# Attention A of a transformer block: the writes of the position rows issued by ACT instead of SP

## The chip, the cores and the metric

The kernel runs on one core of a Trainium2 chip. The metric is the device time of one execution in microseconds (us); less is better. The core has TensorE (PE), VectorE (DVE), ScalarE (ACT), GpSimd (POOL) and SyncE (SP), each with its own instruction stream, and 16 DMA engines that move data between the on-chip memory (SBUF) and the device memory (HBM). Matmul results lie in PSUM, in banks of 512 float32 per partition. The engines meet only through semaphores.

## The reference

Four sequences of 2048 rows of width 256 go through attention A, a feed-forward, attention B (causal) and the feed-forward again, each behind a layer norm and added to the residual. The change touches attention A, which has a relative position term:

```python
score = (einsum('bhsp,bhtp->bhst', q + u, k) + relative_shift(einsum('bhsp,htp->bhst', q + v, pos))) / sqrt(16)
out   = einsum('bhst,bhtp->bhsp', softmax(score), val)          # 16 heads of 16, s = t = 2048

def relative_shift(x):                                          # x: b, h, s, s
    x = pad(x, one zero column on the left)                     # rows of s + 1
    return x.reshape(b, h, s + 1, s)[:, :, 1:, :].reshape(b, h, s, s)
```

The shift is a change of row length: rows written with a pitch of 2049 elements are read back with a pitch of 2048.

## The kernel before

A loop over the four sequences holds nine phases with a meeting of all engines between them. In attention A one head is 16 tiles of 128 query rows by 2048 keys, and a sequence has 16 heads, so 256 tiles, and 1024 in the whole run. Tiles are a software pipeline: in step s the engines work on tiles that lie at different distances ahead of s (`R_LEAD` 9, `Z_LEAD` 6, `C_LEAD` 4, `T_LEAD` 2, `V_LEAD` 1).

What happens to one tile n, in order:

- PE makes the position scores of tile n in four chunks of 512 columns (L522, in step n-9: chunk 3 first, then 0, 1, 2). DVE copies chunk 3 from PSUM into the ring `rel` (L693), ACT copies chunks 0, 1 and 2 (L639). The ring has four slots (`RING`), and both wait for `rel_out` of tile n-4 before they write.
- The 128 rows of `rel`, 1 MB, are written to HBM with a row pitch of 2049 elements (`write_rows`, L758 to L765, in step n-9; the semaphore is `rel_out`).
- In step n-6 the shifted rows, 1 MB, are read back into the ring `z` (`read_shifted`, L743 to L756, semaphore `rel_in`). This waits until PE has transposed the tile that held the slot (`t_full[3]` of tile n-4) and until the writes of tiles n and n+1 have landed.
- In step n-4 PE makes the content scores (L534), DVE adds them onto `z` and takes the maximum (L658), POOL subtracts it (L716).
- In step n-2 PE transposes the tile in four groups (`turn`, L541) and ACT takes the exponential of each (L631) into `pT`. The transposes and the position scores share three banks of PSUM (`R_BANK`, `T_BANK`), so PE waits in turn for ACT's exponentials and copies. Then the values (L562), the sum over four row groups (L550) and the division follow.

ACT's order in a step is: four exponentials of tile s+2, then three copies of tile s+9. DVE's is: low half of the scores, the copy of chunk 3, high half, and small work. SP's is: the read of tile s+6, the write of tile s+9, and in 13 of 16 steps parts of the loads for the next heads (64 KB each, `qu`/`k` and `qv`/`pos`, 24 in a head, and one of 256 KB for the values). Before the change every DMA of the kernel is issued by SP, so all of them are in one queue. SP works in order: when the read of a tile waits, the write behind it in the program waits too.

Of the kernel before, what the change touches and what calls it, by code (L numbers as in the profile page):

```python
# [26 lines left out]
P = 128  # L27
# [4 lines left out]
S = 2048  # L32
NT = S // P
# [9 lines left out]
FLAT = S * (S + 1)  # L43
RING = 4
# [10 lines left out]
R_ACT = [0, 1, 2]  # L55
R_DVE = 3
R_FIRST = 3
HB = 4
NB = 2
# [5 lines left out]
Z_LEAD = 6  # L65
R_LEAD = 9
# [13 lines left out]
def program(nc, a, out, nb=4, nh=H):  # L80

    ctx = ExitStack()
    with ctx:
        def sb(name, shape, dt=F32):
            return ctx.enter_context(nc.sbuf_tensor(name, shape, dt))
# [4 lines left out]
        def sem(name):  # L90
            return ctx.enter_context(nc.semaphore(name))
# [8 lines left out]
        rel_d = nc.dram_tensor("rel_rows", (NB, FLAT), F32).ap()  # L100
# [8 lines left out]
        rel = sb("rel", [P, RING, S])  # L109
# [105 lines left out]
        r_copied = [sem(f"r_copied{c}") for c in range(4)]  # L215
        rel_out = [sem(f"rel_out{k}") for k in range(RING)]
# [14 lines left out]
        def settle(e):  # L231

            e.sem_inc(waited, 1)
# [257 lines left out]
        def in_order(e, b, step):  # L491

            def counts(p):
                return Counts(*(e.snap(b * (nh // HB * per) + p * per)
                                for per in (G, G // OB, 16 * G // RING, HB // NB * QK_INC, HB // NB * 16)))

            with e.Fori(0, 1) as p:
                base = counts(p)
                for s in range(-R_LEAD, 0):
                    step(p, base, s, lambda n: n >= 0)  # L500
            with e.Fori(0, GROUPS - 1) as p:
                base = counts(p)
                for s in range(G):
                    step(p, base, s, lambda n: True)
            with e.Fori(GROUPS - 1, GROUPS) as p:
                base = counts(p)
                for s in range(G):
                    step(p, base, s, lambda n: n < G)

        def moved(base, n):  # L510

            return base.moves + 16 * (n // RING + 1)
# [107 lines left out]
        def act_attn_a(e, b):  # L620

            def step(p, base, s, here):

                r, t = s + R_LEAD, s + T_LEAD
                if here(t):
                    if s >= 0:

                        e.wait_ge(AA["pv_done"], base.tiles + (t - 1))
                    for q in range(4):
                        e.wait_ge(t_full[q], base.tiles + (t + 1))  # L630
                        e.activation(pT[:, t % 2, q * CH:(q + 1) * CH], rg[:, T_BANK[q], :], ACT.Exp,  # L631
                                     scale=SCALE).then_inc(p_ready[q], 1)
                if here(r):
                    if s >= 0 or r >= RING:

                        e.wait_ge(rel_out[r % RING], moved(base, r - RING))
                    for c in R_ACT:
                        e.wait_ge(r_full[c], base.tiles + (r + 1))
                        e.activation(rel[:, r % RING, c * CH:(c + 1) * CH], rg[:, R_BANK[c], :],  # L639
                                     ACT.Copy).then_inc(r_copied[c], 1)  # L640

            in_order(e, b, step)

# [81 lines left out]
        def load_pair(e, q, k, q_src, k_src, h, slots, done):  # L725

            for a in slots:
                load_part(e, q, q_src, h, a, QPART[a], done)
                load_part(e, k, k_src, h, a, KPART[a], done)

        def load_v(e, h, hd, done):
            e.dma_start(v_s[hd].rearrange("p t w -> p (t w)"),
                        v_d[bass.ds(h, 1)].rearrange("a p w -> (a p) w")).then_inc(done, 16)

        def sp_attn_a(e, b):

            every = range(SLOTS)
            load_pair(e, qv_s[0], pos_s[0], qv_d, pos_d, 0, every, qv_loaded[0])
            load_pair(e, qu_s[0], k_s[0], qu_d, k_d, 0, every, AA["qk_loaded0"])
            load_v(e, 0, 0, AA["v_loaded0"])  # L740
            load_pair(e, qv_s[1], pos_s[1], qv_d, pos_d, 1, every, qv_loaded[1])

            def read_shifted(p, base, n, fresh, last):  # L743

                k, hd, i0 = n % RING, n // NT % NB, n % NT * P
                if not fresh:

                    e.wait_ge(t_full[3], e.snap(base.tiles + (n - RING + 1)))
                    settle(e)
                e.wait_ge(rel_out[k], e.snap(moved(base, n)))  # L750
                settle(e)
                if not last:
                    e.wait_ge(rel_out[(n + 1) % RING], e.snap(moved(base, n + 1)))
                    settle(e)
                shifted = bass.AP(tensor=rel_d.tensor, offset=hd * FLAT + (i0 + 1) * S, ap=[[S, P], [1, S]])
                e.dma_start(z[:, k, :], shifted).then_inc(rel_in[k], 16)  # L756

            def write_rows(p, base, n):  # L758

                k, hd, i0 = n % RING, n // NT % NB, n % NT * P  # L760
                for c in (R_DVE, R_ACT[-1]):
                    e.wait_ge(r_copied[c], e.snap(base.tiles + (n + 1)))
                    settle(e)
                there = bass.AP(tensor=rel_d.tensor, offset=hd * FLAT + i0 * (S + 1) + 1, ap=[[S + 1, P], [1, S]])
                e.dma_start(there, rel[:, k, :]).then_inc(rel_out[k], 16)  # L765

            def next_heads(p, base, s, final):

                hd, at = s // NT, s % NT
                nxt = (hd + 1) % NB  # L770
                if at in range(1, 7) and not (final and hd + 1 >= HB):
                    if at == 1:
                        e.wait_ge(AA["hi_ready"], e.snap(base.tiles + hd * NT + C_LEAD))
                        settle(e)
                    load_pair(e, qu_s[nxt], k_s[nxt], qu_d, k_d, e.snap(p * HB + (hd + 1)), (at - 1,),
                              AA[f"qk_loaded{nxt}"])
                if at == 7 and not (final and hd + 1 >= HB):
                    e.wait_ge(AA["pv_done"], e.snap(base.tiles + (hd * NT + V_LEAD)))
                    settle(e)
                    load_v(e, e.snap(p * HB + (hd + 1)), nxt, AA[f"v_loaded{nxt}"])  # L780
                if at in range(8, 14) and not (final and hd + 2 >= HB):
                    if at == 8:
                        e.wait_ge(r_full[2], e.snap(base.tiles + (hd + 1) * NT))
                        settle(e)
                    load_pair(e, qv_s[hd % NB], pos_s[hd % NB], qv_d, pos_d, e.snap(p * HB + (hd + 2)), (at - 8,),
                              qv_loaded[hd % NB])

            def step(p, base, s, here):

                n, r = s + Z_LEAD, s + R_LEAD  # L790
                final = not here(G)
                if here(n):
                    read_shifted(p, base, n, s < 0 and n < RING, n % NT == NT - 1)
                if here(r):
                    write_rows(p, base, r)
                if s >= 0:
                    next_heads(p, base, s, final)

            in_order(e, b, step)

# [394 lines left out]
        def _(e):  # L1196
# [40 lines left out]
            with e.Fori(0, nb) as b0:  # L1237
# [3 lines left out]
                sp_values(e, b, "A")  # L1241
                meet_b(e, b, 2)
                sp_attn_a(e, b)
                meet_b(e, b, 3)
                meet_b(e, b, 4)
# [83 lines left out]
        @block.scalar  # L1329
        def _(e):  # L1330
            e.wait_ge(loaded, 16 * LOADS)
            act_project(e, None, "pos")
            meet(e, None, 0)
            with e.Fori(0, nb) as b:
                meet_b(e, b, 1)
                act_norm(e, b, 0)
                act_project(e, b, "A")
                meet_b(e, b, 2)
                act_attn_a(e, b)
                meet_b(e, b, 3)  # L1340
                act_out(e, b, "A")
                meet_b(e, b, 4)
                act_norm(e, b, 1)
                act_ffn(e, b, 0)
                meet_b(e, b, 5)
                act_norm(e, b, 2)
                act_project(e, b, "B")
                meet_b(e, b, 6)
                act_attn_b(e, b)
                meet_b(e, b, 7)  # L1350
                act_out(e, b, "B")
                meet_b(e, b, 8)
                act_norm(e, b, 3)
                act_ffn(e, b, 1)
                meet_b(e, b, 9)
# [86 lines left out]
```

## Time and profile before

| | |
|---|---|
| median of 3 runs | 11704.78 us (11701.66 to 11712.92) |
| the profiled execution | 11740.77 us, its span 11739.0 us |
| granted clock of TensorE, mean | 0.925 |
| busy share: PE, weight load, DVE, ACT, POOL | 82%, 59%, 53%, 57%, 25% |
| attention A of the first sequence | first write of rows issued at 179.4 us, last at 1833.1 us |

The run repeats the same pattern four times, once for each sequence. In the profile's table of 40 slices the long stretches in which the DMA digits are 9 are the four attention A phases; attention B, which moves few bytes, lies between them. A share of busy time over the whole span is therefore a mean over phases with different limits, and what follows is read phase by phase.

### The profile page before, as it was taken

The page shows a single profiled execution, that of the slowest core. Times are in us where ns is not written, and L with a number is a line of the kernel's source. Part 1 is how long each engine was busy: PE and PEld are TensorE (multiplying, and loading weights), DVE is VectorE, ACT ScalarE, POOL GpSimd, SP SyncE. Part 2 cuts the span into 40 slices and gives each one's busy share as a digit, 9 for nine tenths or more (in the row PEclk, how much of TensorE's full clock was granted, in tenths as well). Part 3 has the DMA queues.
Part 4 walks back from the last instruction along what each step waited for, and adds up shares of the span by engine and source line. Part 5 has one row for each costly group of instructions (what it writes and reads, how often), then busy time and mean ns, then how long its engine had stood idle before and what let it go on. Part 6 is the DMA issues. An engine that isn't in the chain of part 4 may idle for free. (4 is left out here: it accounts for less than half of the span.)

```text
span 11739.0 us, 268351 instructions
## 1 busy us (share of the span) xinstructions
PE 9666.4 (82%) x95520; PEld 6878.1 (59%) x95520; DVE 6260.3 (53%) x14730; ACT 6698.0 (57%) x11009; POOL 2935.3 (25%) x3520
## 2 busy tenths in 40 slices
PE   5887888899687788899968878889986787888999
PEld 3555556666455556566635555556664555555666
DVE  3555553675355555376445555537744555553764
ACT  3665664675365666366546656637744565663764
POOL 2333332001233333200123333320012333332001
PEclk8999999899799999999979999999998999999999
DMA  6999993100699999210079999920007999992000
GB/s 233 337 337 335 345 342 118 49 23 19 216 356 328 334 355 346 102 27 24 17 242 339 341 335 344 339 96 25 24 26 256 338 332 326 346 345 86 24 24 26
DMA packets 452690, 2482.16 MB, mean 211 GB/s; under 512 B 78976, under 2 KB 100992, under 8 KB 188864
## 3 DMA queue, kind: packets, MB, share of 16 engines
q1 hardware_dynamic: 451264, 2463.71, 62.1%
q8 instruction: 826, 13.53, 0.5%
q14 instruction: 600, 4.92, 0.1%
HBM read 1280.34 MB, written 1183.07 MB: 210 GB/s over the span
## 5 line engine op out<-in xcount | busy, mean ns | idle before, releaser
L658 DVE CUSTOM_DVE_ANT_0 z<-sc,z 128x1024 f32<-128x1024 f32 x2048 | 2497.0, 1220 | 2356.4 <-DMA z<-rel_rows 1959.4
L716 POOL TENSOR_SCALAR z<-z,nmax 128x1024 f32<-128x1024 f32 x2048 | 2271.2, 1120 | 4649.0 <-DVE nmax L668 4649.0
L631 ACT ACTIVATE pT<-rg 128x512 f32<-128x512 f32 x4096 | 2445.2, 598 | 855.0 <-PE rg L541 796.3
L639 ACT ACTIVATE rel<-rg 128x512 f32<-128x512 f32 x3072 | 1727.0, 596 | 1895.0 <-PE rg L522 1886.7
L522 PE MATMUL rg<-pos_s,qv_s 96*128 96x512 bf16 x4096 | 1646.3, 410 | 1382.2 <-DVE rel L693 1261.7
L541 PE MATMUL rg<-ident,z 128*128 128x128 f32 x16384 | 2597.7, 283 | 87.6 <-issue 78.6
L541 PEld LDWEIGHTS rg<-ident,z 128*128 128x128 f32 x16384 | 2067.8, 146 | 827.4 <-ACT rel L639 259.9
L522 PEld LDWEIGHTS rg<-pos_s,qv_s 96*128 96x128 bf16 x4096 | 487.6, 120 | 1872.7 <-DVE rel L693 1505.8
L1006 DVE CUSTOM_DVE_ANT_0 z<-sc,mask 128x1024 f32<-128x1024 f32 (+7 forms) x1536 | 1359.3, 910 | 229.2 <-PE sc L825 176.0
L945 ACT ACTIVATE pT<-rg 128x512 f32<-128x512 f32 (+3 forms) x1792 | 928.3, 550 | 776.2 <-PE rg L878 763.3
L953 ACT ACTIVATE z<-z,nmax 128x128 f32<-128x128 f32 (+15 forms) x1024 | 1226.7, 1198 | 90.0 <-POOL nmax L971 78.2
L878 PE MATMUL rg<-ident,z 128*128 128x128 f32 x8704 | 1262.6, 290 | 0.0
L562 PE MATMUL op<-pT,xnT 128*32 128x128 f32 x32768 | 1209.3, 292 | 0.0
L878 PEld LDWEIGHTS rg<-ident,z 128*128 128x128 f32 x8704 | 976.1, 145 | 256.5 <-issue 188.7
L562 PEld LDWEIGHTS op<-pT,xnT 128*32 128x32 f32 x32768 | 899.0, 116 | 262.8 <-issue 213.9
L859 PE MATMUL op<-pT,xnT 128*32 128x128 f32 x17408 | 794.3, 284 | 149.1 <-ACT pT L945 45.0
L693 DVE COPY rel<-rg 128x512 f32<-128x512 f32 x1024 | 702.4, 686 | 184.6 <-PE rg L522 141.6
L859 PEld LDWEIGHTS op<-pT,xnT 128*32 128x32 f32 x17408 | 503.8, 111 | 298.7 <-DVE attn L981 120.7
L534 PE MATMUL sc<-k_sb,xnT 96*128 96x512 bf16 x2048 | 652.3, 401 | 0.0
L534 PE MATMUL sc<-xnT 96*128 96x512 bf16 x2048 | 636.0, 392 | 12.6 <-DVE mlo L658 12.6
L700 DVE COPY po_sb<-op 128x128 f32<-128x128 f32 x1024 | 298.9, 292 | 597.6 <-PE op L562 596.7
L1025 DVE COPY pT<-rg 128x512 f32<-128x512 f32 (+3 forms) x768 | 428.7, 558 | 302.2 <-PE rg L878 293.1
(93 smaller groups left out, 8191.7 us busy)
## 6 DMA issues: line engine op xcount, KB each, us to landing
rel_rows<-rel SPq DMA_DIRECT2D x1024, 1024.0 KB, 11.3
z<-rel_rows SPq DMA_DIRECT2D x1024, 1024.0 KB, 9.1
xnT<-qu_parts SPq DMA_DIRECT2D x792, 64.0 KB, 2.3
xnT<-v_heads SPq DMA_DIRECT2D x132, 256.0 KB, 4.2
v_heads<-rel SPq DMA_DIRECT2D x8, 4096.0 KB, 12.5
k_sb<-k_parts SPq DMA_DIRECT2D x408, 64.0 KB, 2.3
qv_s<-qv_parts SPq DMA_DIRECT2D x384, 64.0 KB, 9.5
pos_s<-pos_parts SPq DMA_DIRECT2D x384, 64.0 KB, 10.4
```

What stands on the lines that cost most here:

```text
L522: e.matmul(rg[:, R_BANK[c], :], qv_s[hd][:, i0:i0 + P], pos_s[hd][:, c * CH:(c + 1) * CH], start=True, stop=True).then_inc(r_full[c], 1)
L534: mm = e.matmul(sc[:, c, :], qu_s[hd % NB][:, i0:i0 + P], k_s[hd % NB][:, c * CH:(c + 1) * CH], start=True, stop=True)
L541: mm = e.transpose(rg[:, T_BANK[q], (j - 4 * q) * P:(j - 4 * q + 1) * P], z[:, n % RING, j * P:(j + 1) * P], ident[:, :])
L562: mm = e.matmul(po[32 * g:32 * g + 32, :], v_s[hd % NB][:, j, :], pT[:, n % 2, j * P:(j + 1) * P], start=j < 4, stop=j + 4 >= NT)
L631: e.activation(pT[:, t % 2, q * CH:(q + 1) * CH], rg[:, T_BANK[q], :], ACT.Exp, scale=SCALE).then_inc(p_ready[q], 1)
L639: e.activation(rel[:, r % RING, c * CH:(c + 1) * CH], rg[:, R_BANK[c], :], ACT.Copy).then_inc(r_copied[c], 1)
L658: e.tensor_tensor_reduce(out=zs, in0=scf[:, 2 * half * CH:2 * (half + 1) * CH], in1=zs, scale=1.0, scalar=-3.0e38, op0=ALU.add, op1=ALU.ma ...
L716: e.tensor_scalar(zs, zs, 1.0, nmax[:, n % 2:n % 2 + 1], ALU.mult, ALU.add).then_inc(AA[done], 1)
L859: mm = e.matmul(po[32 * g:32 * g + 32, :], v_s[t // NT % NB][:, j, :], pT[:, t % 2, j * P:(j + 1) * P], start=j < 4, stop=j + 4 >= nj)
L878: mm = e.transpose(rg[:, B_BANK[q], (j - 4 * q) * P:(j - 4 * q + 1) * P], z[:, t % RING, j * P:(j + 1) * P], ident[:, :])
L953: e.activation(z[:, s % RING, 0:w], z[:, s % RING, 0:w], ACT.Exp, bias=nmax[:, s % 2:s % 2 + 1], scale=SCALE).then_inc(BB["exp_done"], 1)
L1006: e.tensor_tensor_reduce(out=z[:, s % RING, c0:c1], in0=scf[:, p0:p0 + c1 - c0], in1=mask[:, S - width + c0:S - width + c1], scale=1.0, sc ...
```

## The change

`write_rows` moves from SP's program to ACT's. ACT issues it at the end of its part of a step, behind its own last copy of the tile, and on its own DMA queue. The two semaphores that it waits for are the same (DVE's copy of chunk 3 and ACT's copy of chunk 2), and so are the bytes and their places. SP keeps the reads and the loads.

```diff
@@ act_attn_a
                         e.activation(rel[:, r % RING, c * CH:(c + 1) * CH], rg[:, R_BANK[c], :],
                                      ACT.Copy).then_inc(r_copied[c], 1)
+                    write_rows(base, r)
+
+            def write_rows(base, n):
+
+                k, hd, i0 = n % RING, n // NT % NB, n % NT * P
+                for c in (R_DVE, R_ACT[-1]):
+                    e.wait_ge(r_copied[c], base.tiles + (n + 1))
+                settle(e)
+                there = bass.AP(tensor=rel_d.tensor, offset=hd * FLAT + i0 * (S + 1) + 1, ap=[[S + 1, P], [1, S]])
+                e.dma_start(there, rel[:, k, :]).then_inc(rel_out[k], 16)
@@ sp_attn_a
-            def write_rows(p, base, n):
...
@@ sp_attn_a, step
-                n, r = s + Z_LEAD, s + R_LEAD
+                n = s + Z_LEAD
                 final = not here(G)
                 if here(n):
                     read_shifted(p, base, n, s < 0 and n < RING, n % NT == NT - 1)
-                if here(r):
-                    write_rows(p, base, r)
                 if s >= 0:
                     next_heads(p, base, s, final)
```

ACT, two steps in the middle of attention A, before (`pT<-rg` is an exponential, `rel<-rg` a copy of position scores; L638 is a semaphore's value being worked out):

```order
L631 ACTIVATE pT<-rg 128x512 [waits t_full3]
L638 REGISTER_ALU [waits rel_out2]
L639 ACTIVATE rel<-rg 128x512 [waits r_full0]
L639 ACTIVATE rel<-rg 128x512 [waits r_full1]
L639 ACTIVATE rel<-rg 128x512 [waits r_full2]
L630 REGISTER_ALU [waits A_pv_done]
L631 ACTIVATE pT<-rg 128x512 [waits t_full0]
```

and the same place now:

```order
L631 ACTIVATE pT<-rg 128x512 [waits t_full3]
L638 REGISTER_ALU [waits rel_out2]
L639 ACTIVATE rel<-rg 128x512 [waits r_full0]
L639 ACTIVATE rel<-rg 128x512 [waits r_full1]
L639 ACTIVATE rel<-rg 128x512 [waits r_full2]
L650 DMA rel_rows<-rel 128x2048 [waits r_copied3,r_copied2]
L630 REGISTER_ALU [waits A_pv_done]
L631 ACTIVATE pT<-rg 128x512 [waits t_full0]
```

The DMA and its two waits stand between the last copy of one step and the first exponential of the next.

SP, the middle of attention A, before (`z<-rel_rows` is the read of shifted rows, the 16x2048 rows are loads for the next head):

```order
L756 DMA z<-rel_rows 128x2048 [waits t_full3,rel_out0,rel_out1]
L762 REGISTER_ALU
L765 DMA rel_rows<-rel 128x2048 [waits r_copied3,r_copied2]
L722 DMA xnT<-qu_parts 16x2048
L722 DMA xnT<-k_parts 16x2048
L756 DMA z<-rel_rows 128x2048 [waits t_full3,rel_out1,rel_out2]
L762 REGISTER_ALU
```

and now:

```order
L766 DMA z<-rel_rows 128x2048 [waits t_full3,rel_out0,rel_out1]
L732 DMA xnT<-qu_parts 16x2048
L732 DMA xnT<-k_parts 16x2048
L758 REGISTER_ALU
L766 DMA z<-rel_rows 128x2048 [waits t_full3,rel_out1,rel_out2]
```

The write and its wait are gone from between the reads; reads and loads keep their order.

## Rows read from the trace of the kernel before

**Rows 1.** The page's slices: busy tenths of the DMA engines, and their GB/s
```profile
DMA  6999993100699999210079999920007999992000
GB/s 233 337 337 335 345 342 118 49 23 19 216 356 328 334 355 346 102 27 24 17 242 339 341 335 344 339 96 25 24 26 256 338 332 326 346 345 86 24 24 26
```
**Rows 2.** Busy time by stretch: two of attention A, then one of attention B
```profile
core 0: us, PE busy (x) PEld busy (x) DVE busy (x) ACT busy (x) POOL busy (x), PEclk, DMA share, GB/s
600.00:1200.00 600.00, 481.74 (x5252) 344.65 (x5242) 322.56 (x680) 361.27 (x635) 200.88 (x182) 0.93 0.98 335
1200.00:1800.00 600.00, 484.93 (x5413) 347.04 (x5416) 332.67 (x700) 371.31 (x653) 206.29 (x186) 0.96 1.01 344
1900.00:2400.00 500.00, 445.63 (x3805) 315.77 (x3807) 269.39 (x721) 273.95 (x395) 61.50 (x147) 0.94 0.12 39
```
**Rows 3.** Who waited for whom, whole run: total us, times, longest us
```profile
DVE z L658 <- DMA z<-rel_rows: 1959.4, 820, 9.4
ACT rel L639 <- PE rg L522: 1886.7, 1776, 11.2
DVE z L658 <- PE sc L534: 394.9, 222, 12.7
```
**Rows 4.** The same view for SP's queue, whole run
```profile
SPq L233 <- DMA rel_rows<-rel: 2376.5, 903, 6.7
SPq L233 <- ACT rel L639: 1048.5, 837, 4.2
SPq L233 <- PE rg L541: 841.7, 763, 9.0
```
**Rows 5.** The page's DMA issues: KB each, median us from issue to landing
```profile
rel_rows<-rel SPq DMA_DIRECT2D x1024, 1024.0 KB, 11.3
z<-rel_rows SPq DMA_DIRECT2D x1024, 1024.0 KB, 9.1
...
qv_s<-qv_parts SPq DMA_DIRECT2D x384, 64.0 KB, 9.5
```
**Rows 6.** The tile rel_rows: issue ns min/median/max, first and last start
```profile
L765 SPq DMA_DIRECT2D rel_rows<-rel x1024: 314/325/1315, 179.4 to 10584.1; - x171
```
**Rows 7.** Tile rel_rows, window 1700 to 1900 us, same columns
```profile
L765 SPq DMA_DIRECT2D rel_rows<-rel x21: 319/320/326, 1704.7 to 1833.1; - x21
```
**Rows 8.** SP's timeline at the start of attention A
```profile
179.42 2.12 SPq L765 DMA_DIRECT2D rel_rows<-rel  x3
187.45 0.32 SPq L756 DMA_DIRECT2D z<-rel_rows  x1
188.02 0.32 SPq L765 DMA_DIRECT2D rel_rows<-rel  x1
191.01 0.32 SPq L756 DMA_DIRECT2D z<-rel_rows  x1
```
**Rows 9.** DMA from 178 to 218 us, one slice a microsecond
```profile
GB/s 103 115 369 418 401 401 393 451 246 377 246 49 279 188 336 426 418 197 164 270 303 393 442 401 156 164 139 205 426 418 410 254 246 262 319 401 426 459 188 262
```
**Rows 10.** Timeline around a step at 900 to 926 us
```profile
902.33 0.33 SPq L756 DMA_DIRECT2D z<-rel_rows  x1
...
904.49 0.80 PE L541 MATMUL rg<-ident,z 128*128 128x128 f32 x4
...
909.91 0.60 PE L541 MATMUL rg<-ident,z 128*128 128x128 f32 x4
910.11 0.60 ACT L639 ACTIVATE rel<-rg 128x512 f32<-128x512 f32 x1 [0.68 <-PE rg L522]
...
910.61 0.60 ACT L631 ACTIVATE pT<-rg 128x512 f32<-128x512 f32 x1
...
910.79 0.32 SPq L765 DMA_DIRECT2D rel_rows<-rel  x1
...
911.27 1.23 DVE L658 CUSTOM_DVE_ANT_0 z<-sc,z 128x1024 f32<-128x1024 f32 x1 [1.15 <-DMA z<-rel_rows]
...
911.45 1.26 ACT L631 ACTIVATE pT<-rg 128x512 f32<-128x512 f32 x2 [0.25 <-PE rg L541]
911.47 0.60 PE L541 MATMUL rg<-ident,z 128*128 128x128 f32 x4
```

More of the change, by code:

```diff
@@ L756, in read_shifted @@
                 e.dma_start(z[:, k, :], shifted).then_inc(rel_in[k], 16)
-            def write_rows(p, base, n):
[L760 to L765, printed above, removed]
             def next_heads(p, base, s, final):
```

## The prediction

> **What bounds the kernel now.** I read the page's slices first. Where the DMA digits are 9 the bytes run at 326 to 356 GB/s; four such stretches make up more than half of the run [rows 1]. They are the attention A phases. By stretch, the DMA engines are busy for 0.98 to 1.01 of attention A against 0.12 in attention B, while PE is at 481.74 of 600 us (0.80) and ACT at 361.27 (0.60) [rows 2]. So the 16 DMA engines are the full resource of attention A, and PE has a fifth to spare.
>
> The waits say the same. DVE, which opens a tile's work, waits for the shifted rows 820 times in 1024 tiles, 1959.4 us in all; for PE it waits 222 times, 394.9 us [rows 3]. ACT's copies wait 1886.7 us for PE [rows 3], which is the same stall handed on. On SP's side the read waits 903 times for a write to land (2376.5 us), and 763 times for PE's transposes to free its slot (841.7 us); the write waits 837 times for ACT's last copy (1048.5 us) [rows 4]. A write lands 11.3 us after its issue and a read after 9.1 us [rows 5].
>
> The pitch of a tile: the first sequence's first write is issued at 179.4 us [rows 6] and its last at 1833.1 us [rows 7], 255 pitches, so 1653.7/255 = 6.485 us. Per tile the DMA moves two times 1,048,576 bytes, and a sixteenth of a head's loads (24 of 65,536 and one of 262,144 bytes, 114,688): 2,211,840 bytes. Over 6.485 us that is 341 GB/s, which is what rows 2 show (335 and 344). The pitch is thus the bytes over the rate. With 11.3 + 9.1 = 20.4 us of landings in a pitch of 6.485, three transfers are in flight on average. A latency that gets shorter or longer by a microsecond therefore buys nothing by itself: only the rate does.
>
> The rate is not constant. At the start of attention A SP issues three writes and then, from 187.45 us, a read and a write in turn [rows 8]. In 1 us slices the three writes alone run at 418, 401, 401, 393, 451, a mean of 413. From 186 us, when the first read is queued behind them, the rate swings with a period of about 7 us, the pitch of these first tiles: 426 418, then 197 164 270 303; 393 442 401, then 156 164 139 205; 426 418 410, then 254 246 262 319 [rows 9]. Every tile has a fast part of about 3 us and a slow part of about 4 us. That row is the heart of the matter: with undisturbed 413 GB/s the same bytes would take 5.36 us, so 6.485 - 5.36 = 1.13 us of each pitch are lost in the slow parts.
>
> **The change, part by part.** Removed from SP: 1024 issues of 0.325 us [rows 6] and their waits. SP was waiting, not working (2376.5 + 1048.5 + 841.7 us of waits in rows 4), so this gives nothing directly. The write was issued at 910.79 us in a step whose last copy by ACT ended at 910.11 + 0.60 = 910.71 us [rows 10]: 0.08 us later. In 837 of 1024 tiles the write waited for that copy and for nothing else [rows 4], so it can't start earlier than it does; in the other 187 it stood behind a waiting read or loads and starts earlier, but with three transfers in flight this only lengthens its time in the queue. I count 0.
>
> Added to ACT: a wait for its own last copy, and an issue. The trace shows no issue by ACT; the nearest row is SP's, 0.325 us in the median and 1.315 us at most [rows 6]. Before, the first exponential began at 910.61, 0.10 us before the copy's end. Now it begins at about 910.71 + 0.08 + 0.33 = 911.12, so 0.5 us later and ends at 911.72. PE's third group of transposes, which needs the bank of this exponential, began at 911.47 [rows 10] and would begin 0.25 to 0.3 us later. Queued behind the write on ACT are all four exponentials, and behind these the transposes, the values and the next position scores. This falls into DVE's waits for the read in 820 tiles. It is in the open in the 222 tiles where DVE waits for PE: 222 x 0.3 = +67 us. Bounds: 0 us (the queue of transfers absorbs it also there), and 1024 x 0.3 = +307 us if the cover is gone in every tile. I take +67 because DVE's waits for the read, 1.9 us per tile (1959.4/1024), cover the rest. DVE's copy of chunk 3 is no new wait: PE starts chunk 0 in the same bank only after it.
>
> Moved: the order in which bytes are served. Today one queue holds write, read, write, read, each of 1 MB, and the slow part comes once in each such turn [rows 8, 9]. With two queues that are both filled, reads and writes are interleaved in small pieces and there is no turn from 1 MB of writes to 1 MB of reads. I read the slow part as a cost of that turn: it is not there with writes alone, and after the turn the stream reaches the full 426 GB/s again although reads and writes still alternate. While one direction is held up, the other queue has bytes that can move. The gain is bounded by the loss, 1.13 us per tile. It is also bounded by PE: two steps in a row that were hardly held up begin their first group of transposes at 904.49 and 909.91 [rows 10], 5.42 us apart; with what ACT adds a floor of 5.5 to 5.7 us, so at most 6.485 - 5.5 = 0.98 us, 1024 x 0.98 = -1004 us. From the other side the loss may grow (the second rival). I take half of the bound, rounded, 0.5 us: 1024 x 0.5 = -512 us. Half, since the trace shows that the loss is tied to the turn but not how much of it comes from reads and writes being under way together, which will be the case all the time.
>
> The Trainium skill has a rule that speaks against this gain. DMA: Bandwidth & Descriptors, section "Issuing engines are not separate DMA queues", says that DMAs from several engines end up on the same 16 engines and interleave, so that issuing from more than one saves only the sequencer's time. By this rule the sum would be 0 to +67 us, since SP's time is not what is missing. The trace bears out that the 16 engines are full (share 0.98 to 1.01), but no row shows two queues of data at once. The same page, section "Queues, rings and completion order", says that an engine takes turns between its queues at packet granularity; that is the interleaving assumed above, and no run so far shows it here.
>
> Sum: -512 + 67 = -445 us on the profiled execution, 11740.77 - 445 = 11296. The median of the runs shown is 36 us below that execution, so 11,260 us. Every other phase is untouched.
>
> **The rivals.**
>
> *Same rate, other order.* The DMA engines take as long for a byte as before, whatever the queue. For it: they are at 0.98 to 1.01 busy [rows 2], and the total in flight is set by the rings of four tiles, which stay. Against it: the same engines reach 413 GB/s when undisturbed [rows 9]. Time: 11,705, or up to 67 us more with ACT's part. It is also the result if the writes still come out behind the reads in practice, so that the change does nothing of what it says.
>
> *Mixing is the slow state.* The slow parts are then not a cost of the turn, but of reads and writes being at the HBM together, and two queues make this permanent. For it: the slow slices begin while a write is still being served. Against it: the stream recovers within 4 us each time. Price: the slow slices of rows 9 average (197+164+270+303+156+164+139+205+254+246+262+319)/12 = 223 GB/s. A pitch of 6.485 us with 2.21 MB is then about 2.4 us at 223 and 4.1 us at 413, 0.54 and 1.67 MB. If half as much again moves at the slow rate, 0.81/0.223 + 1.40/0.413 = 7.02 us, +0.54 us per tile, +550 us: 12,260. It decides from the point at which the rate with both queues filled falls below 341 GB/s. Doubling the slow bytes would give 7.6 us, beyond 12,800, which I hold for unlikely.
>
> *ACT becomes the path.* The rate stays, and the issue by ACT is longer than by SP or blocks while the reads and loads are being issued; 0.3 us come into the open in most tiles: up to +307 us, 12,010. For it: issues of up to 1.315 us [rows 6]. Against it: ACT is idle for 0.4 of attention A [rows 2].
>
> **How the numbers follow.** Turn cost shrinks, faster: 0.52, own range 10,850 to 11,600. Same rate: 0.17, of which 0.15 within 0.2% and 0.02 just above. Mixing slow: 0.20. ACT's path: 0.11. A change of 0.2%, 23 us, is about what a measurement of this kernel can tell from none. So faster 0.52, same 0.15, slower 0.33. The range reaches down to 10,850 (0.8 us per tile returned) and up to 12,260, the price of the mixing rival; both signs are open, and this is what makes it wide. The time is that of the likeliest case, 11,260.
>
> **What would show it.** Right: in attention A the GB/s of slices above 356, a pitch near 6.0 us, DVE's wait for the read well below 1.9 us per tile, PE's busy share near 0.87, and 1 us slices without the swing between 420 and 200. ACT's first exponential should start about 0.5 us after the last copy's end. Wrong: the rate at 340 GB/s or below with two queues in the page's list. If the rate is the same and the time longer, ACT's exponentials must show as the releaser of PE's transposes far more often than now. If the rate falls, DVE's waits for the read grow and mixing is the cause.

## The result and the profile after

The changed kernel takes 11837.15 us in the median of four runs (11821.67 to 11842.85), the kernel before 11703.22 us. The ratio is 1.0122, with a 95% interval of 1.0103 to 1.0141: slower by 134 us, where 11,260 us, a gain, was forecast. The time lies inside the stated range of 10,850 to 12,260 us, but on the other side of the kernel before; the upper part of the range came from rivals and not from the sum.

The page's slices and its queues after the change. The first two rows answer to [rows 1]; q10 is ACT's queue:

```profile
DMA  6999993100699999311079999931107999993100
GB/s 239 339 323 326 343 340 120 52 24 18 239 328 326 328 336 330 117 41 27 17 245 334 323 324 347 331 108 32 26 17 245 341 330 323 331 339 110 30 24 26
...
q1 hardware_dynamic: 303808, 1389.90, 36.6%
q10 hardware_dynamic: 147456, 1073.81, 25.1%
```

The change did what it says: 1073.81 MB, the writes, run on a queue of their own. But the slices of attention A stay at 323 to 347 GB/s, where slices above 356 were the sign of a gain. The long stretches, with the columns of [rows 2]:

```profile
600.00:1200.00 600.00, 484.81 (x5098) 336.61 (x5097) 316.22 (x660) 345.72 (x615) 195.67 (x176) 0.91 0.97 324
1200.00:1800.00 600.00, 490.81 (x5342) 336.72 (x5340) 329.96 (x692) 363.62 (x645) 204.56 (x184) 0.96 0.99 341
```

Against [rows 2] each has 0.01 to 0.02 less DMA share (the busy share of the 16 DMA engines) and fewer bytes. Over a longer stretch, 400 to 1600 us, before and then after:

```profile
400.00:1600.00 1200.00, 968.28 (x10614) 693.22 (x10614) 652.69 (x1374) 729.22 (x1281) 405.88 (x366) 0.94 1.00 339
```
```profile
400.00:1600.00 1200.00, 978.74 (x10462) 677.06 (x10451) 647.91 (x1354) 710.06 (x1262) 401.07 (x361) 0.93 0.98 334
```

POOL does two instructions per tile, so 183 tiles became 180.5, a pitch of 6.56 us became 6.65. 0.09 us on 1024 tiles would be 93 us; the two profiled executions are 81 us apart, the medians 134. Divide GB/s by the share: 339/1.00 = 339 before, 334/0.98 = 341 after. The same stretch in the three later sequences has 342, 339 and 336 GB/s at shares of 1.00, 1.00 and 0.99 before, and 330, 332 and 331 at 0.98, 0.98 and 0.97 after; over all four it is 339.8 before and 339.4 after. While they are busy, the engines move bytes as fast with two queues as with one; what is new is that they are idle for 2%.

The swing between fast and slow slices was to go away too. In 1 us slices from 900 to 940 us, before and then after:

```profile
GB/s 299 401 418 410 389 242 274 401 406 406 420 336 217 236 383 424 438 393 422 279 360 377 299 356 418 250 360 401 446 336 365 303 361 360 418 426 320 238 258 287
```
```profile
GB/s 344 434 365 287 205 229 328 406 410 393 205 291 250 397 426 432 373 303 305 332 401 422 348 328 246 205 197 234 381 414 430 221 213 246 393 442 426 414 361 340
```

It is still there: from 217 to 446 before, from 197 to 442 after.

The waits after, as in [rows 3]:

```profile
DVE z L668 <- DMA z<-rel_rows: 1803.3, 632, 17.5
ACT rel L639 <- PE rg L522: 1574.5, 1519, 17.8
...
DVE z L668 <- PE sc L534: 625.0, 575, 12.0
PEld rg L541 <- POOL z L726: 566.6, 789, 1.1
...
ACT pT L631 <- ACT rel L639: 460.7, 846, 0.9
```

SP's queue, as in [rows 4], and the landings, as in [rows 5]:

```profile
SPq L233 <- PE rg L541: 4194.8, 999, 16.4
...
SPq L233 <- DMA rel_rows<-rel: 771.8, 515, 4.7
```
```profile
rel_rows<-rel ACTq DMA_DIRECT2D x1024, 1024.0 KB, 9.9
z<-rel_rows SPq DMA_DIRECT2D x1024, 1024.0 KB, 10.7
```

Three things are to be seen. DVE waits for the read in fewer tiles (632 for 820) but longer, 2.9 us instead of 2.4. A write now lands 1.4 us sooner and a read 1.6 us later. And the issue of the read waits in 999 of 1024 tiles for the z slot, which PE's last transposes free (763 before); behind that it waits in 515 tiles for the landing of a write (903 before), 1.5 us each. So in about half of the tiles the slot is now the last thing that the read waits for.

ACT's and SP's place in a step at 903 us, to set beside [rows 10]:

```profile
903.37 0.60 ACT L639 ACTIVATE rel<-rg 128x512 f32<-128x512 f32 x1 [0.34 <-PE rg L522]
...
904.06 0.33 ACTq L650 DMA_DIRECT2D rel_rows<-rel  x1
...
904.50 1.09 ACT L631 ACTIVATE pT<-rg 128x512 f32<-128x512 f32 x2 [0.54 <-ACT rel L639]
```

The first exponential starts 1.13 us after the last copy's start, before it was 0.50 (910.11 and 910.61). So it is 0.63 us later, where 0.5 was forecast. PE feels it: its transposes waited for an exponential 8 times before and 539 times after, 0.36 us each.

```profile
PE rg L541 <- ACT pT L631: 4.3, 8, 0.7
```
```profile
PE rg L541 <- ACT pT L631: 196.4, 539, 0.7
```

This is the sign that the prediction named for "same rate and a longer time".

### The profile page after: what moved, and what is told of

Read it like the earlier page. It is cut to its first block and busy times, and to the rows that moved or that the text cites. A ratio compares the mean times of both kernels' runs of the same rounds, so it can differ in the third digit from the quotient of the medians.

```text
span 11820.1 us, 267199 instructions
## 1 busy us (share of the span) xinstructions
PE 9797.4 (83%) x95520; PEld 6840.6 (58%) x95520; DVE 6289.6 (53%) x14730; ACT 6658.2 (56%) x11009; POOL 2943.7 (25%) x3520
## 3 DMA queue, kind: packets, MB, share of 16 engines
q10 hardware_dynamic: 147456, 1073.81, 25.1%
## 5 line engine op out<-in xcount | busy, mean ns | idle before, releaser
L631 ACT ACTIVATE pT<-rg 128x512 f32<-128x512 f32 x4096 | 2352.1, 596 | 1316.7 <-PE rg L541 846.6
L541 PEld LDWEIGHTS rg<-ident,z 128*128 128x128 f32 x16384 | 1973.6, 146 | 1350.5 <-POOL z L726 566.6
L877 PEld LDWEIGHTS rg<-ident,z 128*128 128x128 f32 x8704 | 965.8, 144 | 252.4 <-issue 187.7
## 6 DMA issues: line engine op xcount, KB each, us to landing
pos_s<-pos_parts SPq DMA_DIRECT2D x384, 64.0 KB, 10.4
```

What stands on the lines that cost most here:

```text
L541: mm = e.transpose(rg[:, T_BANK[q], (j - 4 * q) * P:(j - 4 * q + 1) * P], z[:, n % RING, j * P:(j + 1) * P], ident[:, :])
L877: mm = e.transpose(rg[:, B_BANK[q], (j - 4 * q) * P:(j - 4 * q + 1) * P], z[:, t % RING, j * P:(j + 1) * P], ident[:, :])
```

## The experiments

Two theories at first. ACT: the loss comes from what ACT does in front of its exponentials. Queue: it comes from reads and writes sharing the engines by turns. Chips differ (the kernel before took from 11,490 to 11,703 us on those used), so each run is given by its ratio to the kernel before on the same chip, and two runs are divided by each other only where they ran together. In the cuts of code `...` stands for lines left out.

**ACT's cost with a small DMA.** Writes stay on SP.

```diff
+ for c in (R_DVE, R_ACT[-1]): e.wait_ge(r_copied[c], base.tiles + (r + 1))
+ ...                                  # from the fifth tile on, also a wait for the small DMA of tile r-4
+ e.dma_start(tiny_d[r % RING], ident[0:16, 0:1]).then_inc(tiny_out[r % RING], 16)     # on ACT, behind its copies
```

> The kernel before, writes of the position rows still issued by SP, but ACT also waits for its own last copy and issues a DMA of 16 x 4 bytes from a constant tile to a scratch tensor at the place where the changed kernel issues the write. Theory ACT (the loss of 134 us comes from the wait and the issue, 0.5 us in front of the exponentials): 11,800 to 11,850 us, with ACT's exponentials waiting for its own copy in some 850 tiles as after the change. Theory queue (the loss comes from reads and writes sharing the engines by turns, which makes the reads land later): within 25 us of 11,703.

Measured: 1.0332 (1.029 to 1.0374), more than the change itself. It looked like a proof of theory ACT, but it holds two changes, the delay of ACT and 1024 small DMAs; the next run takes them apart.

**ACT's cost without a DMA.** The same place, but an idle copy:

```diff
+ for c in (R_DVE, R_ACT[-1]): e.wait_ge(r_copied[c], base.tiles + (r + 1))
+ ...
+ e.activation(spare[:, :], ident[:, :], ACT.Copy)
```

> The kernel before with all DMAs on SP's queue. ACT waits for its own last copy and then does an idle copy of 128 x 128 (about 0.3 us) in place of a DMA issue. It is the earlier run with the small DMA (3.3% slower) without any DMA from ACT. Theory ACT: 1.010 to 1.035 of the kernel before, ACT's exponentials behind its copy as after the change. Theory queue: 0.998 to 1.004, and the 3.3% came from the small DMAs.

Measured: 0.9994 (0.9982 to 1.0006). ACT's timeline:

```profile
904.98 0.60 ACT L640 ACTIVATE rel<-rg 128x512 f32<-128x512 f32 x1 [0.65 <-PE rg L523]
905.68 0.31 ACT L645 ACTIVATE spare<-ident 128x128 f32<-128x128 f32 x1
905.90 1.07 ACT L632 ACTIVATE pT<-rg 128x512 f32<-128x512 f32 x2
```

The exponential starts 0.92 us after the copy's start, 0.42 us later than before and two thirds of the delay of the change, and the time does not move. With one queue and the engines full, this delay is covered. It is a milder one than that of the change, though: PE's transposes waited for an exponential 15 times here and 539 times after the change. So the run does not show that the full 0.63 us would be covered. The 3.3% come from the small DMAs, or from them and the delay together.

**The small DMA on SP instead.**

```diff
  e.dma_start(there, rel[:, k, :]).then_inc(rel_out[k], 16)
+ ...                                  # the same wait for the small DMA of tile n-4
+ e.dma_start(tiny_d[k], ident[0:16, 0:1]).then_inc(tiny_out[k], 16)                    # on SP, behind the write
```

> The kernel before, with a DMA of 16 x 4 bytes issued by SP behind each write, on the one queue. The same small DMA on ACT's queue made 3.3%, an equal wait of ACT without a DMA made nothing. Theory second queue (a completion on the second queue holds up the engines): 0.998 to 1.008 here. Theory completions (each small DMA costs by its 16 descriptors and its completion, on whatever queue): 1.02 to 1.035.

Measured: 1.0105 (1.0076 to 1.0134), between the two expectations. A small DMA per tile costs 1% on the queue that is there, and 3.3% on a second one with a delay of ACT.

**The write later in ACT's order.**

```diff
  e.activation(pT[...], rg[:, T_BANK[q], :], ACT.Exp, scale=SCALE).then_inc(p_ready[q], 1)
+ if q == 0 and here(r - 1): write_rows(base, r - 1)
```

> The changed kernel, but ACT issues the write of a tile behind the first exponential of the next step, so no exponential waits for ACT's last copy and the issue falls into a gap in which ACT waits for PE. Two queues remain. Theory ACT: the loss goes, 11,680 to 11,730 us, DVE's waits for PE back to about 220 times. Theory queue: the loss stays, 11,810 to 11,860 us, SP's reads still held by the z slot in nearly all tiles.

Measured: 1.0109 (1.0071 to 1.0147). The exponential is back in its place:

```profile
901.56 0.60 ACT L643 ACTIVATE rel<-rg 128x512 f32<-128x512 f32 x1 [0.61 <-PE rg L522]
902.06 0.60 ACT L631 ACTIVATE pT<-rg 128x512 f32<-128x512 f32 x1
902.54 0.33 ACTq L653 DMA_DIRECT2D rel_rows<-rel  x1
```

PE's transposes wait for an exponential 8 times again, and yet most of the loss stays; a read still lands after 10.4 us, against 8.9 in the run with the idle copy on the same chip. This is against theory ACT as the whole cause. It is not a clean subtraction: the write is issued 0.38 us behind the copy's end and not 0.09, and SP's reads wait for a landed write in 628 tiles, against 467 in the next run. What the later write costs by itself is not known in these leads.

**The change again,** for its ratio beside the later runs.

> The changed kernel once more, on the same chip as the runs beside it, for their ratios. Both theories: 1.010 to 1.014 of the kernel before.

Measured: 1.0153 (1.0115 to 1.0191). That is a little above the 1.010 to 1.014 that were expected. The interval overlaps that of the later write, so ACT's share, 0.4% by the two middle values, is not settled by these two.

**Half reads,** so that the compute engines bound attention A and not the transfers.

```diff
- shifted = bass.AP(..., ap=[[S, P], [1, S]]);      e.dma_start(z[:, k, :], shifted)
+ shifted = bass.AP(..., ap=[[S, P], [1, S // 2]]); e.dma_start(z[:, k, 0:S // 2], shifted)
```

> The kernel before, but each read of shifted rows brings only the first 1024 of the 2048 columns (the rest of z is stale), 1.69 MB per tile in place of 2.21. At 341 GB/s these need 4.95 us, less than the 5.4 us that the engines need, so the engines and not the transfers should bound attention A: pitch 5.3 to 5.5 us, 10,500 to 10,750 us. It is the base for the next run.

> The changed kernel with the same halved reads. With the transfers no longer the bound, what ACT adds must show in full. Theory ACT: 0.1 to 0.3 us per tile above the run with writes on SP, +100 to +300 us. Theory queue: equal to that run within 40 us.

Measured: 0.9137 and 0.9408; medians 10502.6 and 10802.34 us. Where the transfers are not the bound the change costs 300 us, 0.29 us per tile, as much as the 0.3 us that was worked out for ACT, and as theory ACT expected. The second queue is no likely cause here: the reads land sooner than with one queue (5.5 us against 6.3), and ACT's exponentials wait for its own copy in 965 tiles. How much of this price is hidden in the kernel as it is, full reads and all, is open.

**Less compute.** Exponentials of 128 columns, values of 4 blocks, all transfers kept.

```diff
- e.activation(pT[:, t % 2, q * CH:(q + 1) * CH], rg[:, T_BANK[q], :], ACT.Exp, ...)
+ e.activation(pT[:, t % 2, q * CH:q * CH + P], rg[:, T_BANK[q], 0:P], ACT.Exp, ...)
- for j in range(NT):
+ for j in range(4):
...
```

> The kernel before with less compute in attention A: each exponential does 128 of 512 columns and the values only 4 of 16 blocks of keys (results are left out). All transfers stay. The transfers alone should bound attention A: 0.97 to 1.00 of the kernel before. It is the base for the next run.

> The changed kernel with the same lighter compute, so that what ACT adds is covered. It shows what two queues do to the rate of the transfers. Theory ACT: within 0.3% of the light run with one queue. Theory queue: 0.8 to 1.5% above it.

Measured: 1.002 (1.0005 to 1.0035) and 1.004 (1.0015 to 1.0065), a difference of 0.2%. With the same transfers on the same two queues nearly all of the loss is gone. This is what theory ACT expected and theory queue did not. It fits a dependency between read and compute as well: with the short exponentials ACT's issue falls into a gap (its exponentials wait for its copy once in the whole run, 846 times after the change), and the compute has slack for a later read too. What the pair does show is that the second queue does not slow the bytes by itself: 349, 352, 352 and 348 GB/s at a share of 1.01 with one queue, 345, 347, 346 and 346 at 0.99 with two. The read still lands 1.6 us later (10.6 against 9.0), so a later landing costs only where the compute behind it has no slack. That led to a loop of dependencies as the next theory.

**Transposes one step early.** `T_LEAD` 3 and `V_LEAD` 2 in place of 2 and 1, with the waits that this needs: a slot of z is free one step sooner.

```diff
-V_LEAD = 1
-T_LEAD = 2
+V_LEAD = 2
+T_LEAD = 3
...
```

> The changed kernel with the transposes and the values one step earlier (T_LEAD 3, V_LEAD 2), so that a slot of z is free one step earlier and a read is never held up by it. Theory slot (with two queues the read is released only when its z slot is free, lands too late, and the DMA engines run dry for 1 to 2% of the time): the loss goes, 0.990 to 1.003 of the kernel before, DMA busy share back to 1.00, SP waiting for landed writes again and not for PE. Theory rate (two queues move bytes more slowly by themselves): still 1.010 to 1.018.

> The kernel before with the same leads, as the control. With one queue the DMA engines are busy all the time already, so both theories expect 0.995 to 1.005 of the kernel before.

Measured: two queues 1.006 (1.0033 to 1.0087), one queue 0.9947 (0.9917 to 0.9977). Two queues gain from it, but still lose 1.1% against one (11755.72 over 11627.84 us). Two queues, SP's waits:

```profile
SPq L233 <- DMA rel_rows<-rel: 4469.4, 957, 9.0
SPq L233 <- PE rg L541: 310.6, 139, 13.6
```

The slot no longer holds the read, and its other releaser, the landing of a write, has taken over in 957 tiles. That the loss would go was wrong. This pair says more than the change itself, since ACT has no part in it: in these leads ACT's exponentials wait for PE anyway, and for ACT's own copy only 6 times in the whole run. The 1.1% come from the second queue.

**The same with the later write.**

> Two queues, the write issued behind the first exponential of the next step, and the transposes one step earlier. Theory slot: the best of all, 0.985 to 1.000 of the kernel before. Theory rate: 1.008 to 1.013, as with the later write alone.

Measured: 1.0146 (1.011 to 1.0182), where theory slot expected the best time of all. It can be told why: with the slot free the write's landing releases the read (984 tiles), so a write issued later costs 0.7% (11842.32 over 11755.72 us). In the leads of the change, where the slot is the releaser in half of the tiles, the later write showed no loss (1.0109 against 1.0153).

**Free reads, transposes early.** Reads bring rows of an input tensor and wait for no write.

```diff
- e.wait_ge(rel_out[k], ...); e.wait_ge(rel_out[(n + 1) % RING], ...)
- shifted = bass.AP(tensor=rel_d.tensor, ...)
+ shifted = a["embT"][(n % 2) * P:(n % 2 + 1) * P, :]
```

> One queue, transposes one step early, and each read brings 128 rows of 2048 from an input tensor in place of the position rows (the position term is therefore wrong), so no read waits for a write. The base for the next run. The transfers bound attention A as before: 0.98 to 1.00 of the kernel before.

> The same with the writes on ACT's queue. Theory loop (with two queues a write and a read share the engines and end together, and the next read is released only by the landing of a write, so the engines run dry now and then): without this dependency the two queues cost nothing, within 0.3% of the run with one queue. Theory second queue (engines that serve two queues lose time by that alone): 0.8 to 1.4% above it.

Measured: 0.9911 (0.9879 to 0.9943) and 0.9865 (0.9837 to 0.9893). One queue and two:

```profile
400.00:1600.00 1200.00, 1007.40 (x11260) 707.61 (x11257) 691.51 (x1458) 789.45 (x1361) 430.09 (x388) 0.99 1.00 360
```
```profile
400.00:1600.00 1200.00, 1010.36 (x11311) 708.87 (x11312) 694.28 (x1463) 792.99 (x1366) 434.23 (x392) 0.99 0.99 361
...
SPq L233 <- PE rg L541: 4589.9, 1001, 14.0
```

With reads issued early enough two queues cost nothing: 361 against 360 GB/s, and the run with two is the faster by 0.5%. The slot is still what releases the read, in 1001 tiles, but a step sooner: DVE waits for a read only 4 times, against 112 with one queue. One limit of this pair: it is bound by the compute engines. With half of the bytes left out (reads alone and writes alone, below) the same leads take 11,292 and 11,285 us, only 45 to 108 us less than these two. So it shows that a late landing costs nothing where there is slack; it does not show that two queues could carry more.

**Free reads in the leads of the change.** The slot remains, the tie to the writes is gone.

> The kernel before with its own leads, each read bringing 128 rows from an input tensor without waiting for a write (the position term is wrong). Base for the next run: 0.98 to 1.00 of the kernel before.

> The changed kernel with the same free reads, so the tie from a write's landing to a read's issue is gone and what is left is the second queue and ACT's later exponentials. Theory loop: the loss of 1.2 to 1.5% falls to 0.5% or less against the run with one queue. Theory slot (the read held by the z slot is the cause): the loss stays at 1.0% or more, since the slot still holds every read.

Measured: 0.9703 (0.9661 to 0.9746) with one queue, faster than the 0.98 to 1.00 expected, and 1.0032 (1.0018 to 1.0046) with two: 3.6% apart (11520.96 over 11120.14 us). Stretch, landings and SP's wait, one queue:

```profile
400.00:1600.00 1200.00, 1027.57 (x11774) 736.71 (x11773) 723.12 (x1524) 805.52 (x1421) 450.35 (x406) 0.98 1.00 376
...
rel_rows<-rel SPq DMA_DIRECT2D x1024, 1024.0 KB, 9.5
z<-in_embT SPq DMA_DIRECT2D x1024, 1024.0 KB, 9.9
```

and two queues:

```profile
400.00:1600.00 1200.00, 1000.59 (x10751) 692.84 (x10752) 666.59 (x1390) 728.58 (x1299) 410.17 (x370) 0.93 0.98 344
...
SPq L233 <- PE rg L541: 4830.8, 1008, 17.4
...
rel_rows<-rel ACTq DMA_DIRECT2D x1024, 1024.0 KB, 9.3
z<-in_embT SPq DMA_DIRECT2D x1024, 1024.0 KB, 10.6
```

Here the slot holds 1008 reads, no write is waited for, and two queues lose more than in the change itself. The read lands 0.7 us later, and DMA share is 0.98 as after the change. The expectation of theory slot holds for these leads. One transpose step earlier, the same two queues lost nothing.

The 3.6% are not the price of the slot alone. First, ACT's delay is in this pair: with two queues its exponentials wait for its own copy in 903 tiles and PE's transposes for an exponential 608 times (8 with one queue). With one queue the pitch is down to 5.9 us, nearer to the 5.3 us of the run with half reads, where that delay cost up to 300 us; this pair is 401 us apart. Second, the rate while busy fell as well, 376/1.00 = 376 against 344/0.98 = 351 GB/s, so idle engines are not the whole loss. No run parts these.

**Reads alone and writes alone.** One queue, transposes early; the other direction brings 16 of 2048 columns.

> As the run with free reads on one queue, but the writes bring only 16 of 2048 columns. Reads are then nearly alone in attention A. Theory turn (the slow parts are the cost of going from writes to reads): GB/s over the DMA busy share near 413. Theory reads (reads of this shape are slower than writes, with or without writes about): 260 to 320.

> One queue, transposes one step early, reads bring only 16 of 2048 columns, so the writes are nearly alone. Both theories: GB/s over the DMA busy share 380 to 415.

One execution each. Reads alone:

```profile
400.00:1600.00 1200.00, 1017.00 (x11405) 715.10 (x11404) 698.84 (x1473) 798.38 (x1375) 435.89 (x393) 0.99 0.63 193
```

Writes alone:

```profile
400.00:1600.00 1200.00, 1017.03 (x11420) 714.95 (x11419) 700.92 (x1476) 800.34 (x1378) 435.83 (x393) 1.00 0.53 194
```

193/0.63 = 306 GB/s for reads, 194/0.53 = 366 for writes; the first as "theory reads" expected, the second below what both theories expected (380 to 415). The pitch is 1200/196.5 = 6.11 us, so the engines are busy for 3.85 us of a tile with reads and 3.24 with writes, together 7.1 us, or 6.8 without the loads that both runs contain (0.115 MB, 0.3 us). That is no less than the 6.485 us of the mixed stream and looks as if no room were left for a cost of the turn. But these sums can't be trusted: the mixed stream of the free reads in the old leads, the same transfers in turn on one queue, needs only 2.21 MB / 376 GB/s = 5.9 us. A transfer that runs alone has a slow start and end inside its busy time: with reads alone one read shows as 1 us slices of 131, 270, 385 and 262 GB/s. Several queued reads are not slow. From 192 to 197 us of the changed kernel, only SP's queue, reads of position rows and loads, moved bytes:

```profile
DMA packets 294, 2.14 MB, mean 428 GB/s; under 512 B 33, under 2 KB 33, under 8 KB 33
q1 hardware_dynamic: 294, 2.14, 101.3%
```

and from 198 to 202 us both queues moved bytes, still at a mean of 418 GB/s:

```profile
DMA packets 224, 1.67 MB, mean 418 GB/s; under 512 B 20, under 2 KB 20, under 8 KB 20
q10 hardware_dynamic: 123, 0.97, 57.8%
q1 hardware_dynamic: 101, 0.70, 41.3%
```

So in this stretch neither the reads nor the mixture is slow. The run with free reads on one queue has the same turns from writes to reads and, from 900 to 940 us, hardly a slow slice:

```profile
GB/s 336 393 401 393 426 402 336 287 406 422 401 385 430 401 365 418 389 369 434 430 381 389 365 315 385 360 418 418 402 328 332 414 401 426 393 360 381 397 426 410
```

This speaks against the turn as the cause of all the slow slices. What makes them in the kernel before (the rows that are read, the tie of a read to the writes, or something else) stays open.

## Why the prediction was wrong

*What bounds the kernel* was right: with one queue the engines are full, the pitch is bytes over rate, and the time follows the rate.

*SP's issues and waits, 0 us:* nothing speaks against it, but no run takes it alone.

*ACT's part, +67 us:* right in mechanism and nearly in size per tile. The delay was 0.63 us instead of 0.5; where it is in the open the change costs the 0.3 us per tile that was worked out (300 us with halved reads). Its share of the 134 us is open. PE's waits for exponentials, 196 us in all, are new, but part of them falls into waits that were there; an idle copy with two thirds of the delay cost nothing on one queue; and the later write, which takes these waits away, had 1.0109 against 1.0153, with intervals that overlap.

*The step that failed is the order in which bytes are served: "I read the slow part as a cost of that turn", and half of 1.13 us per tile given back, -512 us.* Two queues gave nothing back. The rate while busy is 339.8 GB/s with one queue and 339.4 with two, and the slow slices are still there, down to 197 GB/s. The term measured about 0 instead of -512. The step from "it is not there with writes alone" to the turn was not sound: no row had looked at reads alone, and queued reads alone are fast too, at 428 GB/s. With the turns kept on one queue and only the reads' source and their tie to the writes changed, the stream ran at 376 GB/s; in the run with the idle copy, on a chip that took as long for the kernel before, position rows ran at 353 (mean of four stretches). 2.21 MB at these rates take 5.9 and 6.3 us, so by this estimate some 0.4 us of the 1.13 us belongs to something other than the turn. The row itself was also a poor base. It is the first 40 us of a phase: the rate falls at 186 us, before the first read is issued at 187.45, and the slices from 186 to 192, in which it even falls to 49 GB/s, were passed over. In the middle of attention A, from 900 to 940 us, the swing is milder, with 4 of 40 slices below 250 GB/s.

*What was missing is a loss.* I wrote that the total in flight is what counts and a latency by itself buys nothing. The total did stay, 20.4 us of landings before and 20.6 after. But it shifted: the writes won 1.4 us, for which the reads wait less now (772 us in place of 2377), and the reads lost 1.6 us, for which DVE waits. The read is on a loop with four slots of z: issue, landing, scores two steps ahead of the transposes, the last transposes that free the slot, next issue. My reading is this.
How far is this shown? That a second queue costs even where ACT's exponentials don't wait for its own copies is shown by the pair with early transposes: 1.1%, with the read tied to the write's landing. That it costs nothing where the read has slack is shown by the light compute (0.2%) and by the free reads with early transposes (none). The pair with the slot as the only releaser (3.6%) fits but holds ACT's delay too. How the 134 us of the change itself divide between the later landing and ACT's delay is not shown. Nor does any view show the order of the packets of one engine; the service by turns is an explanation that fits the landings, and the rows from 198 to 202 us show only that both queues move bytes at the same time.

*The rivals.* "Same rate, other order" had the transfers right and was given 0.17; its upper end, 67 us, was ACT's part and not this loop. "Mixing is the slow state" is refuted by the rate while busy, which did not fall. That its price, 12,260 us, made the range wide enough to hold the result is luck. "ACT becomes the path" named a wait that did appear; how much of the time it took is open. The rule of the Trainium skill against the gain (DMA: Bandwidth & Descriptors, "Issuing engines are not separate DMA queues") agrees with these runs: 339.8 GB/s while busy with one queue, 339.4 with two. The runs add that a second queue can cost.

The kernel with one queue, `T_LEAD` 3 and `V_LEAD` 2 was faster than both, 0.9947 (0.9917 to 0.9977) of the kernel before, just beyond the 0.995 that was expected at best.

## What to carry to other kernels

With the DMA engines full, a second queue moved no more bytes here; it changed who waits. Before splitting a queue, find which transfer is on a loop through a small ring of slots, and ask whether later transfers will now share the engines with it and land first. Look also at what stands behind the issue on the engine that takes it over. A fast stretch at the start of a phase is no measure of what a full stream can do, and a transfer that runs alone is none either, since its start and end count as busy. To test whether a switch between two kinds of transfers costs, keep the switches and change something else.

## What the runs showed of the hardware

- One DMA of 16 x 4 bytes per tile on ACT's queue beside the full queue of SP made 1.0332, the same DMA on SP's queue 1.0105, and ACT's wait without it 0.9994. The share was 1.00 in the first of them and the rate 326 to 332 GB/s, so the engines were busy and slower. Why the small one costs more on the second queue was not found.
- At a DMA share of 0.99 to 1.01 on one queue the rate was 336 to 357 GB/s with position rows (kernel before, early transposes, idle copy), and 360 and 376 with free reads from an input tensor, of which the 360 are bound by the compute engines. So a share of 1.00 does not mean that no more bytes could move. Which of the source and the untied issue makes the difference stays open.
- In one queue a small load waits with the large ones: 64 KB landed after 9.5 us in attention A [rows 5], and after 2.2 us at its start in the run with reads alone.
- With the transposes one step early the compute itself is slower: reads alone took 11,292 us in one execution, while the run with halved reads in the old leads took 10502.6. PE's transposes then wait for POOL's subtraction in 1012 tiles. It pays only while the transfers are the bound.
